# Identity products placed ahead of two transposed reads, a chunk scan and a normalised tail in a two-layer kernel on one core

## The reference, cut to what matters

```python
def step(carry, x):
    vec, St = carry
    u, r, c, ca, sa, qt, kt, vt, at, bt = x
    vp = jnp.einsum('bpi,pij->bpj', vec.reshape(b, D // 2, 2), W_block)
    x1, x2 = (vp[..., 0], vp[..., 1])
    rot = jnp.stack([x1 * ca - x2 * sa, x1 * sa + x2 * ca], axis=-1).reshape(b, D)
    vec_new = u * rot + r * c
    pred = jnp.einsum('bhij,bhi->bhj', St, kt)
    delta = vt - pred
    S_new = at[..., None, None] * St + bt[..., None, None] * (kt[..., :, None] * delta[..., None, :])
    read = jnp.einsum('bhij,bhi->bhj', S_new, qt)
    return ((vec_new, S_new), (vec_new, read))
_, (vec_states, reads) = jax.lax.scan(step, (vec0, S0), xs)
m = _rmsnorm(reads, rms_m_w).reshape(b, s, D)      # mean square per head of 8 features
vread = _rmsnorm(vec_states, rms_v_w)              # mean square over 128 features
return (jnp.concatenate([m, vread], axis=-1) @ W_out + b_out) * gate
```

## Time and profile before

| | us |
|---|---|
| median of three executions | 633.51 (632.98 to 635.93) |
| the profiled execution, its time | 638.72 |
| its span, first to last instruction | 637.0 |
| TensorE busy in the span | 582.5 (91%) |
| VectorE busy | 457.9 (72%) |
| ScalarE busy | 427.9 (67%) |
| GpSimd busy | 371.4 (58%) |
| mean granted TensorE clock, share of full | 0.934 |

### The profile page before, as it was taken

The page is one execution under the profiler, slowest core; times in us unless marked ns, Lnnn a source line. Parts: engine busy times, 40 slices in busy tenths (PEclk is TensorE's granted clock), DMA queues, the critical chain, the costliest instruction groups (busy, mean ns, idle before and its releaser), DMA issues.

```text
span 637.0 us, 14542 instructions
## 1 busy us (share of the span) xinstructions
PE 582.5 (91%) x4726; PEld 499.7 (78%) x4726; DVE 457.9 (72%) x1364; ACT 427.9 (67%) x1033; POOL 371.4 (58%) x391
## 2 busy tenths in 40 slices
PE   7999999999998999899998889998976779897996
PEld 6889999599994999769996568786654667576886
DVE  8644567745686558864204898889999999995746
ACT  3375667546765568645685687998888899974441
POOL 5463047502473045725555313949999999978772
PEclk9899999999999999989999987787978898898887
DMA  8965742155412652134322000000000000000002
GB/s 273 334 213 83 196 75 66 51 83 143 82 56 53 148 104 55 54 56 77 72 50 90 1 1 1 1 3 1 1 1 1 0 2 2 1 2 3 1 3 66
DMA packets 104124, 39.86 MB, mean 63 GB/s; under 512 B 85907, under 2 KB 96179, under 8 KB 103923
## 3 DMA queue, kind: packets, MB, share of 16 engines
q1 hardware_dynamic: 98018, 29.34, 20.6%
q0 software_dynamic: 4480, 9.30, 4.3%
q10 hardware_dynamic: 1552, 0.30, 0.2%
HBM read 20.32 MB, written 18.59 MB: 61 GB/s over the span
## 4 chain that ended last, share of the span: by engine, by line
PE 56%; DVE 17%; ACT 11%; issue 6%; POOL 4%; SPq 3%; DMA 2%; DVEq 0%; POOLq 0%; ACTq 0%
PE PS L2364 15%; PE PS L2349 15%; ACT W1s L1965 5%; PE PS L2561 3%; PE PS L2577 2%; SPq L627 2%; PE PS L2264 2%; PE PS L2495 2%; DVE W2s L1420 2%; PE PS L2727 1%; PE PS L2303 1%; DVE PS L1541 1%; PE PS L2742 1%; ACT W2s L2024 1%; DMA xres<-in_L_attn_x_dram 1%
## 5 line engine op out<-in xcount | busy, mean ns | idle before, releaser
L771 POOL DMA_INDIRECT sorted_x<-xrow,pos x93 | 90.2, 970 | 128.5 <-DVE pos L1235 101.0
L2364 PE MATMUL PS<-W2s,wide 128*128 x992 | 139.4, 284 | 0.0
L2349 PE MATMUL PS<-wide,swt 128*128 128x128 f32 x992 | 131.8, 276 | 1.2 <-DVE wide L1300 1.1
L2364 PEld LDWEIGHTS PS<-W2s,wide 128*128 128x128 f32 x992 | 126.7, 191 | 0.5
L2349 PEld LDWEIGHTS PS<-wide,swt 128*128 128x128 f32 x992 | 121.0, 192 | 1.9 <-DVE swt L1294 1.3
L1745 ACT ACTIVATE wide<-PS 128x512 f32<-128x512 f32 x124 | 73.0, 589 | 42.2 <-PE PS L2349 40.9
L1753 ACT ACTIVATE xrow<-PS,tags 128x144 f32<-128x144 f32 (+1 forms) x124 | 46.8, 377 | 41.7 <-PE PS L2364 39.8
L888 POOL TENSOR_TENSOR W1s<-W1s,kT 128x1024 f32<-128x1024 f32 x22 | 52.3, 2383 | 11.6 <-DVE W1s L1559 10.6
L2561 PE MATMUL PS<-ewT,xT 128*128 128x512 f32 x64 | 38.4, 732 | 18.2 <-ACT W2s L2024 18.2
L1303 DVE STREAM_TRANSPOSE wide<-wide 128x128 f32<-128x128 f32 x116 | 33.3, 300 | 30.0 <-DMA wide<-sorted_x 29.1
L1965 ACT ACTIVATE W1s<-W1s,ab 128x128 f32<-128x128 f32 x168 | 51.4, 404 | 3.6 <-DVE W1s L1559 3.5
(11 more groups left out here) (432 smaller groups left out, 1334.2 us busy)
## 6 DMA issues: line engine op xcount, KB each, us to landing
wide<-sorted_x SPq DMA_DIRECT2D x224, 32.0 KB
sorted_x<-wide SPq DMA_DIRECT2D x9, 520.0 KB, 3.4
W1s<-in_L_ffn_W_dram SPq DMA_DIRECT2D x1, 4096.0 KB, 20.1
sorted_x<-wide SPq DMA_DIRECT2D x1, 2015.0 KB, 12.5
sorted_x<-xrow,pos POOLq DMA_INDIRECT x109, 2.7
sorted_x<-wide SPq DMA_DIRECT2D x3, 455.0 KB, 2.9
xres<-in_L_attn_x_dram SPq DMA_DIRECT2D x4, 256.0 KB, 5.0
xrow<-results SPq DMA_DIRECT2D x4, 256.0 KB, 3.9
```

Source lines behind the costliest of these rows:

```text
L771: pool.indirect_dma_start(xs_dram[l + 1][:, :], bass.IndirectOffsetOnAxis(ap=pos[:, t:t + 1], axis=0), xrow[:, t % NR, 0:XW], None).then_i ...
L2349: m = pe.matmul(PS[:, 2 + n, f * P:(f + 1) * P], w1st[:, (c - 1) % WB, f * P:(f + 1) * P], xring[:, (c - 1) % R, :], start=True, stop=True)
L2364: m = pe.matmul(PS[:, 4 + n, 0:w], hTs[:, n, f * P:(f + 1) * P], W2s[:, f * YW:f * YW + (E - 1) * NF + w][:, bass.ds(w2, w)], start=(f == ...
```

## The change

Four idle products (the identity by itself) are put ahead of each of `reads(29)` and `reads(30)`, four ahead of the first join step, five in the tail between `project(0)` and `mean_squares(2)`, and four between `project(1)` and `turn(2)`: 21 in all, 42 MATMUL records. Nothing is removed or moved, and no wait is added. The function `idle_products(n, bank)` exists already (lines 2150 to 2152) and writes the last 128 columns of a PSUM bank.

```diff
-    FILL_AT = {0: 3, 1: 2, 2: 2, 3: 2, 4: 8, 5: 3, 6: 2}
+    FILL_AT = {0: 3, 1: 2, 2: 2, 3: 2, 4: 8, 5: 3, 6: 2, C - 3: 4, C - 2: 4}
...
             pe.wait_ge(trans_ev, 4)
+            idle_products(4, NG - 1)
 
             for c in range(1, NC - 1):
...
             project(0)
+            idle_products(5, 4)
             mean_squares(2)
             mean_squares(3)
             project(1)
+            idle_products(4, 5)
             turn(2)
             turn(3)
             project(2)
```

## The result

The changed kernel took 631.42 us (median of 20 executions, 627.74 to 642.46) beside 634.08 us for the kernel before (20 executions). The ratio is 0.9935, 95% interval 0.9911 to 0.9959; it is taken over the fast executions alone (the one of 642.46 us is left out), so it is not the ratio of the two medians, which is 0.9958. The same kernel was compared with the one before three times more, on other occasions, and gave 0.9984 (0.9953 to 1.0015), 1.0012 (0.9971 to 1.0054) and 0.9992 (0.9960 to 1.0023). Weighted by the widths of their intervals the four give 0.997, with some 0.0015 to either side. But the first does not fit the others, which together give 0.9993 (0.9974 to 1.0013) and show no gain by themselves.

The account below looks back on a forecast made before the run. GpSimd's scan was taken to set the end from 565 to 583 us, then TensorE at half clock to bound the join. Terms 0 + 0 + 0 - 0.6 = -0.6 us gave a median of 632.9 us, range 630.8 to 635.7.

Parts of the forecast that it names:

- The path and the cover: From 565 to 583 us GpSimd's scan sets the end, so twelve products ahead of reads and join cost 0.
- The price of a product: In the join at full clock: 0.16 us a record, 0.32 a product; at half clock 0.29 us a record.
- The tail: From project(0) to VectorE's last sum: nine products delay TensorE but keep the clock full, gain 0.6 us.
- rival B: Tail, clock full anyway: the first mean square waits for useless products, end 1.9 us later, 635.4; chance 0.27.
- The clock behind the wait: Join after GpSimd's scan: the clock falls as before, gain 0; upper end 2.0 us if it stays full.
- rival A: Join keeps its clock behind the shortened wait: 2.0 us more, 630.9, or 629.5 with the later stretch; chance 0.20.
- The rule on idle gaps: Join: by the skill's rule the shortened wait would keep the clock, 2.0 us better; the forecast took 0 instead.

Follow-up runs that it names:

- a2_change_again: The changed kernel once more, all 21 idle products unaltered, against the kernel before: ratio 0.9984 (0.9953 to 1.0015).
- the head's kernel: Only the twelve idle products ahead of reads(29), reads(30) and the first join step, against the kernel before, measured twice: 1.0012 and 0.9996.

## Why the prediction was wrong

- **The path and the cover: right.** From 565 to 583 us GpSimd's scan sets the end, and twelve more products ahead of it cost nothing. The step behind the scan is at 1.40 us after VectorE's first piece in both kernels.
- **The price of a product: wrong, and it matters.** The step that failed was to take 0.16 us a record from a group of four with join pieces on both sides. In a row of eight or ten a record takes 0.11 in the tail and 0.125 at the head. So the join's start moved by 1.5 us instead of 2.1 (565.60 is 5.39 us after the recurrence's end at 560.21; before, 3.90), the wait left was 1.79 us instead of 1.15, and `mean_squares(2)` was held up by about 0.1 us instead of 0.7.
- **The tail: right in mechanism, its term mis-sized.** The clock stayed at full, as forecast. The gain against the profile before was 1.79 us (12.69 to 10.90) where the sum had 0.6. Counted from project(0), the forecast had the first mean square at 2.69 us and the turning at 7.34; they came at 2.11 and 6.13 (617.80 and 621.82, less 615.69). Of these 1.2 us the price explains 0.5 at the first mean square and 0.4 at the turning, 0.9 in all; the rest is that project(0) gave way 0.1 us sooner, and that the mean squares and project(1) took 3.13 us instead of 3.35. The forecast that the same tail at full clock without products would end 2.5 us earlier was right: 12.69 - 10.08 = 2.6. The rival B named the true counterweight, products that bring nothing where the clock holds anyway, but at 0.8 us (10.90 against 10.08) instead of 1.9, and not the first mean square's five but the turning's four were to blame.
- **The clock behind the wait: gain 0 was right for this change.** It fell in all four profiles of it, though the choice rested on one nearest row and rival A had 0.20; the rows did not decide it. What the prediction had wrong is the size of the prize: 2.0 us by VectorE's idle time, where the full clock gives 17.88 - 15.17 = 2.7 us in the first part against this profile and up to 5.6 against those with 20.7 us, and 1.4 to 4.8 us more in the second part, 19.86 against 21.2 to 24.6.
- **The number.** 632.9 us lay in the range with the 631.42 us measured, but as a ratio I forecast 0.999 with nearly all the chance within half a per cent, and the first comparison said 0.9935. With the correct price the tail's term comes to about -1.5 us, and as measured to -1.8, which is 0.997. That all four comparisons together give 0.997 as well agrees with it but is not a proof, as the three repeats alone give 0.9993. The other 2 us of the first comparison were not found again, and no run ties them to the change.
- **The rule on idle gaps.** The Trainium skill (TensorE: Matmul & The Clock Gate, section Why this matters for your kernels) advises keeping long idle gaps from between bursts of matmuls. The traces agree as far as filling the gap goes: with the wait filled whole the clock held in all four profiles. The length of the gap alone doesn't decide here: 1.51 us lost the clock (`a2_change_again`) and 1.74 us kept it. They differ in the work ahead of them, four wide records against 18; that this is the reason fits the runs and was not tested apart.

What stays open is why the stretch at half clock behind the scan is sometimes 10 us and sometimes 27 us long with the same instructions (the head's kernel had both), and whether the head's products change how often the longer one comes; the profiles are too few for that. One thing goes with it: in the five profiles in which the step behind the wait still ran at full (a first group of 0.33 us) the low stretch was 10 us long, and in the seven in which it ran at half (0.48 us) it was 14 to 27.

## What to carry to other kernels

Put idle products directly ahead of the wait that costs the clock, and enough of them (18 records held it, ten did not); wide products more than 10 us earlier, where the clock is full, didn't save it in any of six profiles. Look for the wait by the granted clock of the stretches and by group lengths on either side of it, then price a filler by a row of the same filler, not by a short group mixed with other work. A stretch bound by TensorE at half clock hands over to the next engine once it is at full: here VectorE, at 14.66 of 15.17 us.

Where the clock moves by itself, one comparison of 20 executions can be off by more than its interval says: 0.9935 was followed by 0.9984, 1.0012 and 0.9992. Segments of the profile told the parts apart where the times could not, but a segment too needs several profiles: the join's second part took 19.86 us in one profile of the changed kernel and 21.33 in another.

## What the runs showed of the hardware

The clock was lost with no idle time at all, behind narrow products (from 611 us before; TensorE was busy 4.00 of 4.00 us from 606 to 610). It fell there in four of the 18 profiles, with the same instructions in the others. It was kept through an idle 1.74 us behind 18 wide records. Once lost in the join it stayed low for 10 to 27 us, although TensorE was never idle behind the wait (19.31 of 20.72 us busy in the head's profile, the rest being the wait); that work is mostly 64 by 64 pieces, and that they are the reason was not tested apart. A MATMUL record of the identity on 128 columns in float32 takes 0.11 us in a row, while beside the join's pieces a group of four takes 0.64 us.
